# Moving the second layer's state-space block from the attention stream into the scan stream

## What is computed

```python
xn = layernorm(x)
s  = selective_scan(xn, forward) + selective_scan(xn, backward)   # 16 states each way
g  = silu(ffn(xn) * router_weight)
x  = x + s * g
xn = layernorm(x)
s  = ssd_block(xn)          # rotary, rmsnorm, conv of 4 taps, chunked state space, gated rmsnorm
g  = silu(two_attention_layers(xn))   # 8 heads, windows of 64, each with a gelu FFN
x  = x + s * g
```

## Time and profile before

| | |
|---|---|
| time, median of 3 runs | 4658.02 us (4657.6 to 4661.66) |
| the profiled execution's own time | 4646.64 us |
| its span, first to last instruction | 4644.8 us |
| instructions in it | 53,531 |
| mean granted clock of TensorE in it | 0.881 |

### The profile page before, as it was taken

One profiled execution on the slowest core, in us unless ns is written; L12 is line 12 of the kernel. 1 busy time (PEld: TensorE's weight loads), 2 busy tenths in 40 slices (PEclk: granted clock), 3 DMA queues, 4 the chain that ended last, 5 costly groups with the idle time before them and its releaser, 6 DMA issues. The chain is left out here.

```text
span 4644.8 us, 53531 instructions
## 1 busy us (share of the span) xinstructions
PE 3574.7 (77%) x16160; PEld 1947.4 (42%) x16160; DVE 2898.1 (62%) x4687; ACT 2356.1 (51%) x4102; POOL 1755.3 (38%) x1428
## 2 busy tenths in 40 slices
PE   5777777878777777777777787778787877778776
PEld 1244344444444444344443444444344444444443
DVE  6575665757657575665756657566574765757544
ACT  3455555555555555455555555555554554545444
POOL 2253442525325253342534415244252532525332
PEclk9798889989989898888988988899898888979888
DMA  1000000000000000000000000000000000000000
GB/s 74 3 1 1 5 1 5 1 1 5 1 6 1 1 5 1 6 1 6 1 1 6 1 6 1 1 6 1 6 1 1 6 1 6 1 1 3 1 3 3
DMA packets 18378, 20.44 MB, mean 4 GB/s; under 512 B 768, under 2 KB 17152, under 8 KB 17792
## 3 DMA queue, kind: packets, MB, share of 16 engines
q1 hardware_dynamic: 18048, 16.44, 1.1%
HBM read 12.24 MB, written 4.19 MB: 4 GB/s over the span
## 5 line engine op out<-in xcount | busy, mean ns | idle before, releaser
L1392 POOL TENSOR_TENSOR hc<-hst,Cs 128x512 f32<-128x512 f32 x512 | 649.9, 1269 | 1735.9 <-DVE hst L1157 1721.2
L1157 DVE TENSOR_TENSOR_SCAN hst<-dA,bx 128x512 f32<-128x512 f32 x512 | 752.2, 1469 | 313.9 <-issue 164.6
L493 PE MATMUL bank<-hc,C 128*128 128x512 f32 x1024 | 581.8, 652 | 6.9 <-POOL hc L1392 6.9
L517 PE MATMUL bank<-W,xs 128*128 128x512 f32 x960 | 471.4, 628 | 39.0 <-DVE tmp L1298 33.7
L505 PE MATMUL bank<-parts,sel 96*128 96x512 bf16 x1024 | 355.9, 421 | 183.7 <-DVE bx L1149 128.7
L1468 POOL TENSOR_TENSOR Pm<-Pm,rinv 128x512 f32<-128x512 f32 x256 | 273.6, 1069 | 523.3 <-DVE rinv L1314 510.1
L1149 DVE TENSOR_TENSOR bx<-u,bank 128x512 f32<-128x512 f32 x512 | 345.5, 675 | 199.4 <-PE bank L505 170.2
L1453 POOL TENSOR_TENSOR oT<-tmp 128x512 f32<-128x512 f32 x256 | 324.5, 1268 | 273.5 <-DVE tmp L1298 181.8
L864 ACT COPY Cs<-bank 128x512 f32<-128x512 f32 x512 | 294.3, 575 | 244.2 <-PE bank L505 224.1
L983 ACT ACTIVATE Pm<-Pm 128x512 f32<-128x512 f32 x256 | 161.4, 630 | 462.6 <-DVE Pm L1323 462.6
L858 ACT ACTIVATE dA<-delta,neg_a 128x512 f32<-128x512 f32 x512 | 367.9, 719 | 44.1 <-DVE hst L1157 39.2
(11 more groups left out here) (226 smaller groups left out, 6322.8 us busy)
## 6 DMA issues: line engine op xcount, KB each, us to landing
W<-wpack SPq DMA_DIRECT2D x1, 4498.0 KB, 13.6
x_tok<-x SPq DMA_DIRECT2D x16, 256.0 KB, 2.9
out<-xa SPq DMA_DIRECT2D x16, 256.0 KB, 2.2
rot<-tables SPq DMA_DIRECT2D x2, 512.0 KB, 16.3
wc_f<-taps SPq DMA_DIRECT2D x1, 1024.0 KB, 19.7
C<-cpack SPq DMA_DIRECT2D x1, 721.0 KB, 14.9
Pm<-mask SPq DMA_DIRECT2D x1, 320.0 KB, 15.2
tmp<-rowpack SPq DMA_DIRECT2D x1, 256.0 KB, 17.4
```

What stands on the lines that cost most here:

```text
L493: mm(y_acc[:, :], ident, hc[:, k % 2, :], start=(k == 0), stop=(k == 2 * NS - 1))\
L517: mm(b[:, :], weights, rhs, start=True, stop=True).then_inc(full(ring, job), 1)
L1157: v.tensor_tensor_scan(o, a, b, 0.0, ALU.mult, ALU.add).then_inc(sem("a_h"), 1)
L1392: g_.tensor_tensor(hc[:, k % 2, :], hst[:, k % 2, :], Cs[:, k % 2, :], ALU.mult)\
```

## The change

The state-space block leaves stream B and becomes `mamba`, a part of stream A between `head` and the next `prologue`. It is computed for element i in the same round as its scan, in buffers of stream A that nobody needs between scan and prologue (`hst`, `hc`, `bx`, `gate`, `delta`, `u`, `dA`, `Cs`, `dlow`, `xc`). Its result goes over in `sm1` and `smb`. Stream B is the two attention layers alone, so `PACE` spreads A's slots anew: the scan over layer 0, `head` and `mamba` over the units of layer 1, `prologue` over layer 1's FFN. `CUT` is 0, which leaves the code for a split scan unused.

The scan's input is written by VectorE back into the bank that held B; `bx` is no longer its buffer. The bank is then free after the scan (`a_h`) and not after the multiply (`a_bx`).

The rings are three banks each. The state-space block's jobs are on A's ring, where they had four banks of B's.

The residual of the attention layers is kept shifted, in `xs0`: VectorE adds into it in two halves of 64 partitions, and ScalarE's `shifted` copies after `wo` and between the layers are gone.

The core of the diff:

```diff
-          + [job for k in range(2 * NS) for job in ((f"B{k}", "a_bx", k + 1), (f"C{k}", "a_Cs", k + 1))]
+          + [job for k in range(2 * NS) for job in ((f"B{k}", "a_h", k + 1), (f"C{k}", "a_Cs", k + 1))]
...
-B_JOBS = ([("ab0", "m_ld", 1)] + [(f"ab{q}", "m_ea", q) for q in range(1, NT)]
+A_JOBS += ([("ab0", "m_ld", 1)] + [(f"ab{q}", "m_ea", q) for q in range(1, NT)]
...
+CUT = 0
 SCAN = 0
-A_END = SCAN + 2 * NS
+A_END = SCAN + 2 * NS - CUT
 HEAD = A_END + 1
-PRO = HEAD + 8
-A_SLOTS = PRO + 9
-LAYER = 11
+MAMBA = HEAD + 8
+PRO = MAMBA + 11
+SCAN1 = PRO + 9
+A_SLOTS = SCAN1 + CUT
+LAYER = 1
...
-PACE = [(0, 2), (LAYER, 16), (LAYER + UNITS_END, 28), (LAYER + LAYER_SLOTS, HEAD), (LAYER + LAYER_SLOTS + 5, PRO),
-        (LAYER + LAYER_SLOTS + UNITS_END, A_SLOTS - 1), (B_END, A_SLOTS - 1), (B_SLOTS, A_SLOTS)]
+PACE = [(0, 0), (LAYER, 2), (LAYER + UNITS_END, 22), (LAYER + LAYER_SLOTS, HEAD), (LAYER + LAYER_SLOTS + UNITS_END, PRO),
+        (B_END, A_SLOTS - 1), (B_SLOTS, A_SLOTS)]
...
-        rings = {"A": (banks[0:2], A_JOBS), "B": (banks[3:7], B_JOBS)}
+        rings = {"A": (banks[0:2] + banks[3:4], A_JOBS), "B": (banks[4:7], B_JOBS)}
...
-        big1 = kT[:, :, :].rearrange("p q (h l) -> p q h l", h=HM)
-        big2 = oT[:, :, :].rearrange("p q (h l) -> p q h l", h=HM)
-        xbc, sz, y3 = vt[:, 0:4], vt[:, 4:6], PT
+        heads_of = [t.rearrange("p (h l) -> p h l", h=HM) for t in
+                    (hst[:, 0, :], hst[:, 1, :], hc[:, 0, :], bx[:, 0, :], bx[:, 1, :], hc[:, 1, :], gate[:, :])]
+        big1, big2 = [None] + heads_of[0:3], heads_of[3:7]
+        xbc = [delta[:, 0, :], delta[:, 1, :], u[:, 0, :], u[:, 1, :]]
+        sz, ysq, y_r, sm1 = dA, u, xc, sm
...
-                    v.tensor_tensor(bx[:, k % 2, :], u[:, d, :], b[:, :], ALU.mult).then_inc(sem("a_bx"), 1)
+                    v.tensor_tensor(b[:, :], u[:, d, :], b[:, :], ALU.mult).then_inc(sem("a_bx"), 1)
...
-                    o, a, b = hst[:, k % 2, :], dA[:, k % 2, :], bx[:, k % 2, :]
+                    o, a, b = hst[:, k % 2, :], dA[:, k % 2, :], b[:, :]
...
-                    v.tensor_tensor(xa[:, :], xin[:, :], b[:, :], ALU.add).then_inc(sem("f_xa"), 1)
+                    for r, o in HALVES:
+                        v.tensor_tensor(xs0[r, o:o + T], xs0[r, o:o + T], b[r, :], ALU.add).then_inc(sem("f_xs"), 1)
...
-                    shifted(xsA, xa, "f_xs", "f_xa", i, l + 1)
...
-                    if l + 1 < NL:
-                        shifted(xs0, yB, "t_xs", "f_y", i, l + 1)
```

More of the change, by code:

```diff
@@ L393, in finish @@
                 sp.dma_start(dst, xo[:, :].rearrange("p (q d) -> p q d", q=NT)).then_inc(sem("store"), 16)
-            run(sp, prologue, scan, head, stage_b, finish)
+            run(sp, prologue, scan, head, mamba, stage_b, finish)
             sp.wait_ge(sem("store"), NB * 16)
@@ L494, in accumulate @@
                         .then_inc(sem("a_yacc"), 1)
[L496 to L499, removed]
+                yield scan_slot(lo)
+                if lo == 0:
+                    pe.wait_ge(*step("a_parts", i))
+                for k in range(lo, hi):
+                    yield scan_slot(k)
                     d, s = k // NS, k % NS
@@ L568, in stage_b @@
                                   start=True, stop=True)
-                    last.then_inc(full("B", f"ab{q}"), 1)
+                    last.then_inc(full("A", f"ab{q}"), 1)
                 pe.wait_ge(*step("m_h", i))
                 for t in range(4):
[L572 to L577, removed]
+                    yield MAMBA + 2 + t
+                    if used("A", f"cx{t}", i):
+                        pe.wait_ge(*vacant("A", f"cx{t}", i))
+                    b = bank("A", f"cx{t}")
                     for k in range(TAPS):
@@ L718, in stage_b @@
                         n = s - UNIT
+                        if l == 0 and s == 2 and ended is not None:
+                            finish(ended)
                         if s < NT:
@@ L767, in finish @@
                 last.then_inc(sem("xo_full"), 1)
-            run(pe, prologue, scan, head, stage_b, finish)
+            run(pe, prologue, scan, head, mamba, stage_b, finish)
         @block.scalar
@@ L820, in prologue @@
                 yield PRO + 4
+                if later(i):
+                    act.wait_ge(*before("m_sm1", i))
                 for d in range(2):
@@ L849, in prologue, with scan @@
                 tables()
-            def scan(i):
-                yield SCAN
-                act.wait_ge(*step("a_delta", i))
-                for k in range(2 * NS):
-                    yield SCAN + k
+            def scan(i, lo, hi):
+                yield scan_slot(lo)
+                if lo == 0:
+                    act.wait_ge(*step("a_delta", i))
+                for k in range(lo, hi):
+                    yield scan_slot(k)
                     if k >= 2:
@@ L941, in stage_b @@
+            def stage_b(i, ended):
+                yield 0
+                shifted(xs0, xn2, "t_xs", "m_xn", i, 1)
                 for l in range(NL):
@@ L945, in stage_b @@
                         n = s - UNIT
+                        if l == 0 and s == 3:
+                            if ended is not None:
+                                finish(ended)
+                            act.wait_ge(*step("a_x1", i))
+                            nc.scalar.copy(x1b[:, :], x1[:, :]).then_inc(sem("m_x1b"), 1)
                         if s < NT:
@@ L1022, in finish @@
                 nc.scalar.copy(xo[:, :], o_acc[:, :]).then_inc(sem("xo"), 1)
-            run(act, prologue, scan, head, stage_b, finish)
+            run(act, prologue, scan, head, mamba, stage_b, finish)
         @block.vector
@@ L1360, in finish @@
                 pass
-            run(dve, prologue, scan, head, stage_b, finish)
+            run(dve, prologue, scan, head, mamba, stage_b, finish)
         @block.gpsimd
@@ L1379, in prologue, with scan @@
                     .then_inc(sem("a_parts"), 1)
[L1380 to L1385 removed]
+                pool.wait_ge(*step("a_parts", i))
+            def scan(i, lo, hi):
+                if lo == CUT:
+                    prior.clear()
+                for k in range(lo, hi):
+                    yield scan_slot(k)
                     pool.wait_ge(*step("a_h", i, k + 1))
@@ L1396, in head @@
             def head(i):
-                prior.clear()
                 yield HEAD + 2
@@ L1472, in finish @@
                 pass
-            run(pool, prologue, scan, head, stage_b, finish)
+            run(pool, prologue, scan, head, mamba, stage_b, finish)
 SETUP = 7 + 4 + 3 + 2 + TAPS + 1 + 2 + len(TABLES) * NL
```

334 lines of the change are left out of this document (173 added, 161 removed).

## The result

The change makes the kernel slower: 4752.0 us (median of 4, 4751.5 to 4759.4) against 4657.8 (median of 4), a ratio of 1.021, interval 1.019 to 1.023.

What follows compares the result with a forecast made beforehand. No engine is full; how long the two interleaved streams hold each other up counts. Stretches summed to 276.5 us a round against 286.2, -150 over 15 rounds, -16 at the ends: 4658 - 166 = 4492 us, range 4310 to 4650.

Steps and rivals of the forecast that it cites:

- the rings: Three banks each: waits on eight projection slots and the fourth convolution bank cost +1.7 us a round, between 0 and 6.
- The start of the round: Two scan steps behind layer 0's FFN, and layer 0's first projection waiting for the shifted copy: 4 us a round.
- 96.6 + 4: Layer 0's units with 22 scan steps at 1.64 us each on 60.5, 96.6 us, plus 4 for the round's start.
- The base: The round subtracted from: forecast 276.5 us against one cut round of 286.2, giving -10 us a round.
- Layer 1 with its FFN, 149: Layer 1 with head and prologue stays 120.3 us; the block adds 28.6, 0.7 of its 40.8 alone; about 149.
- Rival 3: The block in layer 1 blocks attention; it decides from 0.94 of the block's length; 4837 us at 1.25; chance 0.15.
- The scan, 123 us: Scan with its input in a bank lasts 1.23 us, not 1.469: 123 us less of VectorE over 512 scans.
- Rival 2: The scan is no faster from a bank, staying at 1.47 us: 4628 us; chance 0.12.
- The shifted copies, -1.7: ScalarE's copies gone, VectorE a half-addition more, at three places: 0.5 to 0.6 us saved each, -1.7 a round.
- The ends, -16: Outside the rounds: block alone in front +40.8, none behind -40.8, 32 lone scan steps 0.5 us shorter: -16 us.
- The range: Bounds on layer 0, FFN and block, -17 to +11 us a round, 4240 to 4660; 8 in 10: 4310 to 4650.
- The clock of the last stretch above 0.8: Sign of the forecast: granted clock in layer 1's FFN, 0.77 of full before, rises above 0.8.

Runs made afterwards that it cites:

- e1: The change with B spreads on two of ring A's banks and C spreads on the third: 4583 us, 0.986 of the kernel before.
- e13: The change with the C spread issued ahead of the B spread, banks still in turn and the release still late: 4579 us, 0.985 of the kernel before.
- e6: e4 with the change's shifted residual alone, the block left in the attention stream: 4473 us, 0.962 of the kernel before.
- e10: e1 with 18 instead of 22 scan steps by the end of layer 0's units and 22 side slots by layer 0's end: 4653 us, ratio 1.000.
- e11: e8 with the block's convolution cut from four taps to one, so it computes something else: 4395 us, 0.945 of the kernel before.
- e4: Kernel before with 3+3 banks, B spreads on two banks, C on the third, scan input in PSUM: 4510 us, ratio 0.970.
- e2: The change with the multiply writing SBUF again, so the B bank is free before the scan: 4706 us, 1.013 of the kernel before.
- e3: Kernel before with three banks for each ring, and VectorE's M multiplies ahead of its xdt multiplies: 4625 us, ratio 0.994.
- e8: e1 with 20 instead of 22 scan steps by the end of layer 0's units and 27 side slots by layer 0's end: 4517 us, ratio 0.971.

## Why the prediction was wrong, point by point

**The sum against the result.** Forecast was -10 us a round, measured were +7.6: over 15 rounds 264 us, the whole miss of 260 (the ends and the distance between profiled time and median differ by +7 and -11). The 17.6 us a round are, in the terms below, 10.8 for the late bank, 6.9 for the stretch to layer 0's `wo`, -2.8 for its FFN and 3 for the base.

- **The term that failed: the rings, "+1.7, between 0 and 6".** For ring A I had looked at the fourth convolution bank alone, never at the release that the diff's first line changes, from `a_bx` to `a_h`, and did not count three places back in the list. It is worth 291.0 - 280.2 = 10.8 us a round, 162 us. It alone turns the sign: without it the change is 1.4% faster (e1, e13).
- **The start of the round, within "4".** In e1 the stretch to layer 0's `wo` is 107.5 us, where 96.6 + 4 were forecast: +6.9 us a round; the FFN gave 2.8 of it back (24.2 for 27). Charged to the 22 steps, that would be (107.5 - 4 - 60.5) / 22 = 1.95 a step in place of 1.64. But the rows above show another place for it: VectorE's last part of the prologue, for which the sum had no term here, stands ahead of the first scan, which starts 13.3 us behind the FFN in e1 and 5.2 in e6. These 8 us cover the 6.9. Nor do the balances show a higher price of a step: from e10's 18 to e1's 22 the stretch grows by 6.4 us, 1.6 a step (though by nothing between 20 and 22). No run takes that part of the prologue away alone, so this is read from the rows and not shown by an experiment.
- **The base.** The -10 was taken from the round that I had cut, 286.2 us, while the mean by SP's stores was 283.2, in my own rows. 3 us a round, 45 in all, were never there.
- **Layer 1 with its FFN, 149:** measured 147.2 (148.5 in e1). The sum was right and its parts were not. Without the block, e6 has 92.8 + 17.7 = 110.5 in place of my 120.3, so the block with the rest of the move added 38.0 us in e1, 0.93 of its 40.8 alone, in place of 0.7. With the 8 us of the prologue that now stand at the head of the next round it is 46, 1.13 of its length. Rival 3 named 0.94 as the point from which it decides, and I had it at 0.15. No kernel isolates the block's share; that the block itself blocks attention, as rival 3 had it, is not shown, and e11 speaks against it for the convolution.
- **The scan, 123 us:** right. Its mean is 1221 ns, and VectorE's time in it fell from 752 to 625 us. In the kernel's time e4 gives 115 us for it and e1 against e2 123, each with the split of the banks in it. Steps alone stand 1.85 us apart (scans at 88.94 and 90.79 us of the change; 1.90 was forecast). Rival 2 is out, and the estimate from the Trainium skill (VectorE: DVE Perf Modes, "The TRN2 errata"), 65 ns more a scan from a bank, did not show.
- **The shifted copies, -1.7:** right, 2.0 (e6).
- **The ends, -16:** the sign was right; 104.8 us of span less 15 x 7.6 leave -9.
- **The range.** Its upper end was added up wrong: the bounds given (layer 0 at 100, FFN 31, block 35) are 3.4 + 4 + 6.4 = 13.8 us a round above the forecast, and 18.1 with the rings at 6, where the text has 11. At 18.1 all together the time would be 4764, so the ring term's own upper bound belonged in the sum.
- **The clock of the last stretch above 0.8:** right, 0.94 for 0.77. It gave no time, as that stretch now holds the prologue.

**What each part is worth**, from ratios to the kernel before, as steps from each kernel to the next: rings -0.6% (e3), input in PSUM with the split -2.4 (e4), shifted residual -0.8 (e6), the block moved at the best balance found +0.9 (e8), its balance in the change +1.5 (e1), the late bank +3.5 (the change). They add up to +2.1, as steps of one chain must. Three parts are gains; the one in the title of the change is a loss of 0.9 even at its best here, and the two accidents that came with it cost 5.0.

## What to carry to other kernels

When a buffer's release moves to a later event, don't ask how long it is held: write down, job by job, which earlier job each one must now wait for, in the ring's own order, and what stands behind it in the same queue. Here the order of two tuples was worth 3.5%. When a part moves into a stretch, look on every engine where its last instructions come to stand: here the prologue's were meant to be inside the FFN, and VectorE's stood behind it. A change of several parts is best run part by part: the best kernel had three of the four. Take the base of a difference from the mean round, not from the one that was cut.

## What the runs showed of the hardware

- A scan of 128x512 fp32 with its input in PSUM takes 1220 to 1222 ns, each of the 512 in the change. With both operands in SBUF the shortest takes 1223 and the longest 2868 before, and the mean is 1469 before and 1487 in e2.
- GpSimd gets slower with them: with the scan's input out of SBUF, its rotary multiply went from 1154 to 1063 ns (e3 to e4), and in the moved kernel from 1241 (e2) to 1043 (e1). I had charged it to VectorE alone.
- An addition on 64 of 128 partitions (678 to 694 ns in the change) takes as long as on all 128 (686 to 690 before).
